# Separate stage orders for each engine, and coefficients from powers of one symmetric matrix, in a four-layer graph kernel

## The reference, cut to what matters

```python
def layer0(x): h = relu(x@w1_loop + adj@(x@w1_neigh) + b1)
               h = relu(h@w2_loop + adj@(h@w2_neigh) + b2); return (x + h) * 0.5
def layer1(x): h = x @ fc.T + fc_b; w_eff = (w*clip(d,0,1)) @ w.T      # symmetric
               8 times: h += 1/8 * (sigmoid(alpha)*0.5*(adj@h - h) + h@w_eff - h + x); return h
def layer2(x): x and x scaled by row sums of adj (once, twice), and of softmax(relu(n1@n2)); concat @ W + b
def layer3(x): attention over 256 edges (src, dst): scores, softmax over the edges of one src,
               weighted sum of values of dst, @ W_out
x = layernorm(x + layer(x))   # after each layer
```

## Time and profile before

| | us |
|---|---|
| median of 3 runs | 724.84 (724.22 to 725.11) |
| profiled execution | 727.18 |
| its span, first to last instruction | 725.3 |
| PE busy, share of the span | 597.7, 82% |
| DVE / ACT / POOL busy | 466.0 / 331.2 / 220.2 |
| mean granted PE clock | 0.901 |

### The profile page before, as it was taken

The page is one execution under the profiler, slowest core; times in us unless marked ns, Lnnn a source line. Parts: engine busy times, 40 slices in busy tenths (PEclk is TensorE's granted clock), DMA queues, the critical chain, the costliest instruction groups (busy, mean ns, idle before and its releaser), DMA issues.

```text
span 725.3 us, 9315 instructions
## 1 busy us (share of the span) xinstructions
PE 597.7 (82%) x3024; PEld 504.5 (70%) x3024; DVE 466.0 (64%) x1256; ACT 331.2 (46%) x777; POOL 220.2 (30%) x222
## 2 busy tenths in 40 slices
PE   2768849689999999996885859899999999785662
PEld 2556618558997889974774747789887998674541
DVE  6883677235464576537798779726639662678665
ACT  2661211464725367424285354663544752264132
POOL 1252502252216311232155343450552122302402
PEclk9897758789999999997898999999999999987676
DMA  7100000300000000211031110400000011001122
GB/s 221 33 0 30 0 1 0 117 1 0 2 1 1 1 1 1 83 34 59 3 114 59 58 59 1 117 1 1 1 0 1 1 67 51 0 1 59 58 58 59
DMA packets 28502, 24.61 MB, mean 34 GB/s; under 512 B 3739, under 2 KB 22683, under 8 KB 28453
## 3 DMA queue, kind: packets, MB, share of 16 engines
q1 hardware_dynamic: 27012, 19.25, 8.7%
q0 software_dynamic: 1440, 4.72, 2.1%
HBM read 15.58 MB, written 8.39 MB: 33 GB/s over the span
## 4 chain that ended last, share of the span: by engine, by line
PE 60%; DVE 28%; ACT 5%; issue 3%; POOL 2%; DMA 1%; ACTq 0%; DVEq 0%; POOLq 0%
PE bank L1260 32%; PE bank L1542 11%; DVE stats L1076 6%; PE bank L1459 5%; PE bank L1458 4%; ACT ZH L624 2%; PE bank L1434 2%; PE bank L1446 1%; PE bank L1515 1%; POOL ZL L540 1%; DVE XF L1167 1%; DVE XF L1241 1%; PE bank L1328 1%; POOL small L563 1%; DVE XF L1094 1%
## 5 line engine op out<-in xcount | busy, mean ns | idle before, releaser
L563 POOL TENSOR_TENSOR small<-small,minus_half 128x8 f32<-128x8 f32 x32 | 55.1, 1722 | 314.4 <-DVE small L1069 314.4
L540 POOL TENSOR_TENSOR ZL<-XF,ZH 128x512 fp32r<-128x512 f32 x64 | 80.9, 1299 | 105.8 <-ACT ZH L624 105.8
L624 ACT ACTIVATE ZH<-bank 128x128 fp32r<-128x128 f32 (+1 forms) x112 | 35.8, 323 | 110.4 <-PE bank L1260 109.9
L1048 DVE TENSOR_TENSOR ZL<-bank,ZH 128x128 fp32r<-128x128 f32 (+1 forms) x112 | 37.7, 345 | 69.7 <-ACT XF L624 53.4
L813 ACT ACTIVATE XF<-XF,small 128x128 f32<-128x128 f32 x128 | 52.0, 486 | 53.1 <-POOL small L565 46.8
L1260 PE MATMUL bank<-QH,YR 128*128 128x384 f32 x256 | 75.9, 337 | 0.0
L1459 PE MATMUL bank<-ZL,BTH 128*128 128x512 f32 x192 | 74.3, 418 | 0.0
L1458 PE MATMUL bank<-ZH,BTH 128*128 128x512 f32 x144 | 61.0, 423 | 2.1 <-POOL ZL L540 2.0
L1076 DVE BATCH_NORM_STATS2 stats<-XF 128x6 f32<-128x128 f32 x256 | 55.8, 281 | 2.2
L1542 PE MATMUL bank<-ZH,RH 128*128 128x512 f32 x128 | 51.1, 399 | 1.7 <-POOL ZL L540 0.8
L1542 PE MATMUL bank<-ZH,RL 128*128 128x512 f32 x128 | 50.7, 396 | 0.0
(11 more groups left out here) (280 smaller groups left out, 1535.9 us busy)
## 6 DMA issues: line engine op xcount, KB each, us to landing
XF<-in_x SPq DMA_DIRECT2D x16, 256.0 KB, 3.9
XT<-in_xT SPq DMA_DIRECT2D x16, 256.0 KB, 4.5
x_rows<-XF SPq DMA_DIRECT2D x16, 256.0 KB, 2.6
out_x<-XF SPq DMA_DIRECT2D x16, 256.0 KB, 2.8
XF<-in_adj SPq DMA_DIRECT2D x1, 1024.0 KB, 5.6
Q<-in_L_gnn_W SPq DMA_DIRECT2D x1, 448.0 KB
Z<-x_rows,ends_at POOLq DMA_INDIRECT x16, 3.5
Q<-in_L_gnn_w_neigh SPq DMA_DIRECT2D x2, 64.0 KB, 4.4
```

The lines of the kernel that those rows point to most:

```text
L540: g.tensor_tensor(lo, whole, raw(hi), ALU.subtract).then_inc(pool_done[s], 1)
L563: g.tensor_tensor(sm[:, 6, :], sm[:, 5, :], minus_half[:, :], ALU.pow).then_inc(pool_done[s], 1)
L624: return A.activation(out_, in_, ACT.Copy, **more)
L1048: ins = (v.tensor_tensor(lo, part, raw(hi), ALU.subtract) if shift is None else v.scalar_tensor_tensor(lo, part, shift, raw(hi), ALU.add, ...
```

## The change

1. in_order stays only to number the steps of the preparation (w_numbered). Each engine gets its own list of stages, own_order. For the tensor, scalar and vector lists the stages are the same as before except for powers; their places differ. In the preparation pw0, pw1, pw2 stand in place of powers, spread between neigh1, r2, conv1, edges, pair2 and neigh2, and pair2 and neigh2 of group 0 come before r3. 1.neigh1 on PE stands directly behind w.end and ahead of 0.step1. In the vector list row_sum moves into lmat.
2. Only powers of V are formed, V2, V3, V4 and V5 to V8, in three steps; V is symmetric, so it can be the transposed operand as it is. ACT scales them by binomials into VC (8 blocks). DVE adds them up with 28 scalar_tensor_tensor into SV (8 blocks), which POOL has set to scaled identities. Q_k is fc' times VC_k plus centring times SV_k: 7 products over up to three blocks at once. POOL's stage q and its wait are gone.
3. Scratch moves from X1, T1 and part of TL1 to Y1, F1 and tiles of its own (VC, SV, FJV). `load(1, 1)` has no wait, `load_t(1, 1)` waits for one_hot. In stream 1's first turn x0 waits for l3, conv1 (ACT) for picked and t_sum, pair2 (DVE) for q_t; step1 of group 0 waits for "done". The logits, picked and q_t use stream 0's banks, after conv2 of group 0.

```diff
-        adj_rows = T1[:, NB * N + 2 * E:NB * N + 2 * E + EB * N].rearrange("p (e m) -> p e m", m=N)
-        power_0 = scratch("X1", [3, D])
-        powers = scratch("T1", [(EULER_STEPS - 2) // 2, 4 * D])
+        at["F1"] = 0
+        adj_rows = scratch("F1", [EB, N])
+        power = scratch("F1", [EULER_STEPS - 1, D])
+        FCN, CENTRE, V = FJV[:, 0, :], FJV[:, 1, :], FJV[:, 2, :]
...
+        own_order = {
+            "tensor": """w.adj w.low w.w0 w.v w.pw0 0.neigh1 w.r2 w.pw1 0.conv1 w.edges 0.pair2 w.pw2 0.neigh2 w.r3 w.rt
+                w.l2_mean w.weights w.picked w.soft w.end 1.neigh1 0.step1 0.t1 1.conv1 0.step2 0.tz.0 0.tz.1
+                0.lot.0 0.tz.2 1.pair2 0.lot.1 0.tz.3 1.neigh2 0.lot.2 0.lot.3 0.giant1 1.step1 1.t1 0.giant2
+                1.step2 1.tz.0 0.t2 1.tz.1 0.l2.0 0.l2.1 0.l2.2 0.l2.3 1.lot.0 1.tz.2 1.lot.1 1.tz.3 1.lot.2 1.lot.3
+                1.giant1 0.gather 0.qv 0.score 1.giant2 0.spread 0.wout 1.t2 0.scatter 1.l2.0 1.l2.1 1.l2.2 1.l2.3
+                2.neigh1 2.conv1 2.pair2 2.neigh2 1.gather 1.qv 1.score 2.step1 1.spread 1.wout 2.t1 1.scatter
+                2.step2 2.tz.0 2.tz.1 2.lot.0 2.tz.2 3.neigh1 2.lot.1 3.conv1 2.tz.3 2.lot.2 3.pair2 3.neigh2
+                2.lot.3 2.giant1 3.step1 3.t1 2.giant2 3.step2 3.tz.0 3.tz.1 3.lot.0 3.tz.2 2.t2 3.lot.1 2.l2.0
+                2.l2.1 2.l2.2 3.tz.3 2.l2.3 3.lot.2 3.lot.3 3.giant1 3.giant2 2.gather 2.qv 3.t2 2.score 3.l2.0
+                3.l2.1 3.l2.2 3.l2.3 2.spread 2.wout 2.scatter 3.gather 3.qv 3.score 3.spread 3.wout 3.scatter""",
+            "scalar": """w.adj w.low 0.x0 w.v 0.t0 w.lmat 0.neigh1 w.pw0 w.r2 0.conv1 0.triple w.pw1 0.pair2 w.pw2 w.rt
+                0.norm.0 1.x0 1.t0 w.picked w.soft w.end 0.split1 1.neigh1 0.t1 0.split2 1.conv1 1.triple 0.tz.0
+                0.tz.1 0.lot.0 0.tz.2 1.pair2 0.lot.1 0.tz.3 0.lot.2 0.lot.3 1.norm.0 1.split1 0.split3 1.t1
+                1.split2 0.norm.1 1.tz.0 0.t2 1.tz.1 0.l2.0 0.l2.1 0.l2.2 0.l2.3 1.lot.0 1.tz.2 1.lot.1 1.tz.3
+                0.norm.2 1.lot.2 1.lot.3 0.gather 0.qv 1.split3 0.score 1.norm.1 0.wout 1.t2 1.l2.0 1.l2.1 0.norm.3
+                1.l2.2 2.x0 1.l2.3 2.t0 2.neigh1 2.conv1 2.triple 2.pair2 1.norm.2 2.norm.0 1.gather 1.qv 2.split1
+                1.score 1.wout 2.t1 2.split2 2.tz.0 2.tz.1 1.norm.3 3.x0 2.lot.0 2.tz.2 3.t0 3.neigh1 2.lot.1
+                3.conv1 2.tz.3 3.triple 2.lot.2 3.pair2 2.lot.3 3.norm.0 3.split1 2.split3 3.t1 3.split2 3.tz.0
+                3.tz.1 2.norm.1 3.lot.0 3.tz.2 2.t2 3.lot.1 2.l2.0 2.l2.1 2.l2.2 3.tz.3 2.l2.3 3.lot.2 3.lot.3
+                2.norm.2 3.split3 2.gather 3.norm.1 2.qv 3.t2 2.score 3.l2.0 3.l2.1 3.l2.2 3.l2.3 3.norm.2 2.wout
+                3.gather 3.qv 2.norm.3 3.score 3.wout 3.norm.3""",
+            "vector": """w.adj w.low w.w0 w.v w.lmat w.pw0 0.t0 0.neigh1 w.r2 w.pw1 w.edges 0.pair2 w.pw2 0.neigh2 w.r3 w.rt
+                w.one_hot w.q w.weights w.picked w.soft w.end 0.norm.0 1.t0 1.neigh1 0.step1 0.t1 0.step2 0.tz.0
+                0.tz.1 0.lot.0 0.tz.2 1.pair2 0.lot.1 0.tz.3 1.neigh2 0.lot.2 0.lot.3 1.norm.0 0.giant1 1.step1 1.t1
+                0.giant2 1.step2 0.norm.1 0.t2 1.tz.0 0.l2.0 0.l2.1 1.tz.1 0.l2.2 1.lot.0 1.tz.2 0.l2.3 1.lot.1
+                1.tz.3 0.norm.2 1.lot.2 1.lot.3 0.x3 1.giant1 0.gather 0.qv 0.score 1.giant2 0.spread 1.norm.1
+                0.wout 1.t2 0.scatter 1.l2.0 1.l2.1 0.norm.3 2.t0 2.neigh1 1.l2.2 1.l2.3 2.pair2 1.norm.2 2.neigh2
+                1.x3 1.gather 1.qv 2.norm.0 1.score 2.step1 1.spread 1.wout 2.t1 1.scatter 2.step2 2.tz.0 2.tz.1
+                2.lot.0 1.norm.3 2.tz.2 3.t0 3.neigh1 2.lot.1 2.tz.3 3.pair2 2.lot.2 3.neigh2 2.lot.3 3.norm.0
+                2.giant1 3.step1 3.t1 2.giant2 3.step2 3.tz.0 3.tz.1 2.norm.1 3.lot.0 3.tz.2 2.t2 3.lot.1 2.l2.0
+                2.l2.1 3.tz.3 2.l2.2 3.lot.2 2.l2.3 3.lot.3 2.norm.2 3.giant1 2.x3 3.giant2 2.gather 3.norm.1 2.qv
+                3.t2 2.score 3.l2.0 3.l2.1 3.l2.2 3.l2.3 3.norm.2 2.spread 2.wout 2.scatter 3.x3 3.gather 3.qv
+                2.norm.3 3.score 3.spread 3.wout 3.scatter 3.norm.3""",
+            "gpsimd": """0.x0 0.neigh1 0.conv1 0.stats.0 w.one_hot 1.x0 0.split1 1.neigh1 0.split2 1.conv1 1.stats.0 1.split1
+                0.split3 1.split2 0.stats.1 0.stats.2 0.x3 1.split3 1.stats.1 0.stats.3 2.x0 2.neigh1 2.conv1
+                1.stats.2 1.x3 2.stats.0 2.split1 2.split2 1.stats.3 3.x0 3.neigh1 3.conv1 3.stats.0 3.split1
...
+
+        def run(stages, engine=None):
+
+            for name in own_order[engine].split() if engine else in_order:
...
 
-            def w_end():
-                sync.wait_ge(w_dve_done, after(w_dve_steps, 0, "done"))
-                load(1, 1)
+            load(1, 1)
+
+            def w_one_hot():
+                sync.wait_ge(w_dve_done, after(w_dve_steps, 0, "one_hot"))
                 load_t(1, 1)
...
+            for k in range(EULER_STEPS):
+                link(g.tensor_scalar(SV[:, k, :], ident[:, :], DT + (1.0 if k == 0 else 0.0), None, ALU.mult))
             g.memset(a_pad[:, :], 0.0).then_inc(w_pool_done, 1)
...
-            def w_q():
-                gp.wait_ge(w_dve_done, after(w_dve_steps, 0, "r_lo", NB - 1))
-                for factor in factors:
-                    link(g.tensor_scalar(ident_by[factor], ident[:, :], factor, None, ALU.mult))
-                g.memset(pool_junk, 0.0).then_inc(w_pool_done, 1)
-
-            def w_end():
...
+
+            def by_choice(p, src):
+
+                k = EULER_STEPS - p
+                copy(VC[:, k, :], src, scale=float(comb(EULER_STEPS, k))).then_inc(w_act_done, 1)
...
 
                 ac.wait_ge(x_loaded[s], (turn + 1) * (16 * NB))
+                if (turn, s) == (0, 1):
+                    ac.wait_ge(w_pe_done, after(w_pe_steps, 0, "l3", NB - 1))
                 for a in range(NB):
...
+                v.tensor_reduce(row_sum, adj_sb, AX, ALU.add).then_inc(w_dve_done, 1)
...
+            def w_pw0():
+                dv.wait_ge(w_dve_done, after(w_dve_steps, 0, "row_sum"))
+                dv.wait_ge(w_pe_done, after(w_pe_steps, 0, "v2"))
+                v.tensor_copy(power[:, 0, :], w_bank[3][:, 0:D]).then_inc(w_dve_done, 1)
...
+
+            def w_sums():
+
+                nonlocal n
+                dv.wait_ge(w_pool_done, after(w_pool_steps, 0, "const"))
+                dv.wait_ge(w_dve_done, after(w_dve_steps, 0, "v8"))
+                for p in range(1, EULER_STEPS):
+                    if p > 1:
+                        dv.wait_ge(dve_chain, n)
+                    v_p = V if p == 1 else power[:, p - 2, :]
+                    for k in range(EULER_STEPS - p):
+                        v.scalar_tensor_tensor(SV[:, k, :], v_p, DT * comb(k + p, k), SV[:, k, :],
+                                               ALU.mult, ALU.add).then_inc(dve_chain, 1)
+                        n += 1
+                dv.wait_ge(dve_chain, n)
+                v.memset(tmp_c, 0.0).then_inc(w_dve_done, 1)
...
             def neigh1(turn, s):
+                if (turn, s) == (0, 1):
+                    dv.wait_ge(w_pe_done, after(w_pe_steps, 0, "l2_mean", 1))
...
             def w_r2():
+                pt.wait_ge(w_dve_done, after(w_dve_steps, 0, "v2"))
                 by_adjacency("l")
 
             def w_r3():
-                pt.wait_ge(w_dve_done, after(w_dve_steps, 0, "src_col"))
+                pt.wait_ge(w_dve_done, max(after(w_dve_steps, 0, "src_col"), after(w_dve_steps, 0, "v8")))
...
-                products(w_bank[0][:, 0:D], [(V4, power(4, 0))]).then_inc(w_pe_done, 1)
+            def w_pw0():
+                pt.wait_ge(w_dve_done, after(w_dve_steps, 0, "nv1_t"))
+                products(w_bank[3][:, 0:D], [(V, V)]).then_inc(w_pe_done, 1)
+
+            def w_pw1():
+                pt.wait_ge(w_dve_done, max(after(w_dve_steps, 0, "v2"), after(w_dve_steps, 0, "l2", NB - 1)))
+                products(w_bank[0][:, 0:D], [(power[:, 0, :], V)])
+                products(w_bank[0][:, D:2 * D], [(power[:, 0, :], power[:, 0, :])]).then_inc(w_pe_done, 1)
+
+            def w_pw2():
+                pt.wait_ge(w_dve_done, after(w_dve_steps, 0, "v4"))
+                products(w_bank[3][:, 0:D], [(power[:, 2, :], V)])
+                products(w_bank[3][:, D:4 * D], [(power[:, 2, :], power[:, 0:3, :])]).then_inc(w_pe_done, 1)
 
...
             def w_soft():
+                pt.wait_ge(dve_done[0], after(dve_steps, 0, "conv2", 1))
                 for a in range(NB):
...
             def w_q():
-                pt.wait_ge(w_pool_done, after(w_pool_steps, 0, "q"))
...
+                pt.wait_ge(dve_done[0], after(dve_steps, 0, "conv2", NB - 1))
+                pt.wait_ge(w_dve_done, max(after(w_dve_steps, 0, "log_in"), after(w_dve_steps, 0, "rowmax", NB - 1)))
                 for i in range(LOTS):
-                    for place in range(LOT):
-                        k = place * LOT + i
-                        (_, f_factor), *parts = q_parts[k]
```

(14 more changed lines are left out.)

234 lines of the change are left out of this document (115 added, 119 removed).

## The result

The changed kernel takes 718.97 us (median of 4 runs, 717.28 to 720.04) against 724.97 for the kernel before on the same chip: a ratio of 0.9903, with a 95% interval of 0.9886 to 0.9919. Five further runs in a later study gave 719.6 us and 0.9925 (0.9912 to 0.9938). The forecast was 704, with 694 to 715 for 8 in 10: right in sign, but a gain of 20.5 us was forecast and 6.0 came. The profiled execution took 717.28 us, its span 715.5, PE busy 578.1, DVE 485.9, POOL 222.5 us, clock 0.914.

What follows compares the result with a forecast made beforehand. PE bounds it (60% of the chain of waits, DVE 28%), saturated in two stretches, 118 us idle in the others. 13 + 11 − 1 − 2.5 = 20.5 us of gain from 724.84 gave 704, range 694 to 715 for 8 in 10.

Steps and rivals of the forecast that it cites:

- lead at 0.step2's end: Preparation to 0.step2: step2 ends as before with 13.5 us of stream 1 done; gain 13, ends 9 and 18.
- middle: Old 314 to 458 us: reordered stages remove PE waits, score chain 12 earlier; gain 11, ends 3 and 13.
- end: Behind 3.giant1: 2.gather moves behind 3.giant2, so gather_lo stands behind statistics; loss 2.5, ends 0 and 4.
- 0.step2 to 1.giant1: In front of 0.t2 one place fewer covers the norm: loss 1.
- my walk: Preparation, DVE queue followed stage by stage: sums from 92.7, taking 12.1; PE's products done at 132.8, bounds 128.5 to 136.
- The stretch after it is PE-bound: Behind 0.step2, with DVE at 95 of 169 us: the head start is a gain of 13.
- the middle's queue walk: Middle, DVE's queue in its new order, assuming no wait missed: 1.l2.2 and 1.l2.3 end at 386, score chain 12 earlier.
- new gaps over 5 us in sum: Sign of being wrong, in saturated stretches: the separate orders cost where the forecast put nothing.
- rival (d): Slower, by the port DVE and POOL share: a norm meeting POOL's low parts costs 3.9 more; 739 with 9 more; chance 0.08.
- norms of 6 us: Sign of being wrong: norms on DVE taking 6 us in number.
- The new wait for gather_lo behind 3.giant2: Sign of being right, at the end: PE newly waits for gather_lo, 2.48 us, behind 8 us of statistics.
- Rival (a): Only the lead stays; in the middle what one wait yields returns in the next: 13 + 3 − 3.5 = 12.5, 712; chance 0.22.

Runs made afterwards that it cites:

- old rest: Changed kernel with every engine's stages behind 0.step2 back in the order of the kernel before, new preparation and early stream 1 kept: 716.95 us.
- S and E old: Changed kernel with the old order from 0.step2 to 1.giant1 and from 2.tz.0 on, new order only between: 714.01 us.
- S old: Changed kernel with only the stages between 0.step2 and 1.giant1 back in the old order on each engine: 715.34 us.
- the changed kernel with the late 1.x0: Changed kernel with nothing altered except that POOL's 1.x0 waits for VectorE's picked stage: 714.92 us, ratio 0.9850.
- the preparation alone: Changed kernel with stream 1 starting behind 0.step2 as before and all stages after the preparation in old order: 722.84 us.
- the kernel with the late 1.x0: The 714.01 us kernel (new order only from 1.giant1 to 2.tz.0) with POOL's 1.x0 waiting for VectorE's picked stage: 707.77 us.
- the products inside the softmax: The 707.77 us kernel (POOL's 1.x0 waiting for picked) with the three w.end coefficient products taken into the softmax stage: 707.76 us.

## Why the prediction was wrong

By its own terms, in us of gain: the forecast, the two profiles set side by side, and the medians of kernels that differ in one part (725.37, 722.84, 716.95, 714.01, 715.34 and 719.60, read in the order of the last column):

```
                         forecast   profiles   medians
lead at 0.step2's end      13         11.6       8.4   (preparation 2.5, early start 5.9)
middle                     11          6.4       2.9   (old rest -> S and E old)
2.tz to 3.giant1            0          0        -1.3   (S and E old -> S old, both rows together)
end                        -2.5       -3.5
0.step2 to 1.giant1        -1         -4.6      -4.3   (S old -> changed kernel)
sum                        20.5        9.9       5.7   (span 9.8)
```

Each step of the last column is uncertain by 1 to 2 us; by the ratios it reads 3.4, 5.1, 3.0, -1.3 and -4.8. Of the profiles that of before was 2.2 us above its median and that of after 1.7 below, which is 3.9 of the difference between the two sums. I took the first into account for the level and not for the gain; the second couldn't be known. Against the second profile of before the lead is 9.5 instead of 11.6.

**The preparation: its times right, its worth not.** Edges' answer, pair2, neigh2 and the one-hot stage came 0 to 3.5 us behind my walk (sums start at 96.2, forecast 92.7), the sums took 9.7 instead of 12.1, 1.neigh1 stood behind the seven products without a gap and done was at 134.1 (132.8, bounds 128.5 to 136). One reading in that walk was wrong: the 0.27 us of the earlier trace rows lie between a sum and a tensor_scalar, not between two like instructions. The sums alone take 6.5 us, not 8.2, and the copy and the sums pay 4.2 for POOL's work, not 3.9, so the total came near by two errors of opposite sign. What the lead was worth I read against the profile of before alone: 13, of which 8.4 are left by the medians. The runs price it apart: preparation 2.5, early start 5.9 with POOL beside the sums, and 6.2 more without (by the ratios of each study 3.4, 5.1 and 5.6), so 11 to 12 for the early start when nothing is paid beside it. POOL's x0, in my sum at 3.9, is 4.2 on DVE and 5.6 to 6.2 in the time.

**The failed steps: "The stretch after it is PE-bound", and the middle's queue walk.** The first let the whole head start through a stretch and costed the reordering in it at 1, because PE was full there. It was full because transposes had another stage's work between them and their user. With the 0.l2 stages in a row some of that cover went, and 4.3 us with the new order as a whole, shown by putting the order back (2.2 to 2.9 of it in the late half). That it is the neighbours and nothing else in that order is read from the waits, not tried apart. Another 2.2 us, as the profiles have it, went because 1.neigh1 and 1.conv1, done early, had been such cover themselves. The sign I had named, new gaps over 5 us in sum, came only in part: PE's empty time there rose by 3.4 us, from 1.66 to 5.08.

In the second I walked DVE with the durations of the trace of before, l2.2 and l2.3 in 8 us. They took 14, because POOL's subtractions for group 2 now ran beside them. I had the price of this for the sums and for norm.3 and did not ask which other stages would now meet POOL's; rival (d) asked that of norms only. Leaving POOL's work out gave 6.3 us in the middle's length and 7.7 in the time (7.1 by the ratios), so my 11 was the 2.9 of the medians plus about that. Norm.0 of group 0 took 4.30 us instead of 2.13 too, beside POOL's subtractions and under cover of 1.neigh1; no norm took more than 5.11, so the sign "norms of 6 us" did not come.

The middle's mechanism failed as well as its size. I had PE's empty time fall from 30 to about 20 us. Over the whole middle it is 31.1 and 27.4 in the two profiles of before, and 27.1 to 29.3 in the ten profiles with the new order and POOL's work in it: the waits of 4.62 and 7.66 went, and so did one of 2.54 behind the score chain, but new ones came.

```profile
333.70 3.41 PE L1341 MATMUL bank<-w_out,Y 128*128 128x128 f32 x16 [4.44 <-DVE Y L1312]
```

With this one ahead of 0.wout there are 1.75 and 4.19 us inside 2.pair2, and 7.74 ahead of 1.gather where the kernel before had 5.37 ahead of 1.qv. What fell is PE's busy time for the same 557 matmuls, from 112.1 and 116.8 to between 107.6 and 111.0, with the mean granted clock at 0.91 to 0.94 instead of 0.88 to 0.90. I had no term for that, so the part of the forecast that came in there came in partly by luck.

**The rest.** 2.conv1's wait of 7.66 fell to 0.26 as forecast, and the score chain of group 0 came early. The new wait for gather_lo behind 3.giant2 came: 4.96 us.

```profile
602.61 0.58 PE L1621 MATMUL bank<-ZH,RH 128*128 128x512 f32 x1 [2.67 <-POOL ZL L583]
...
622.31 0.55 PE L1341 MATMUL bank<-TH,gH 128*128 128x256 f32 x1 [4.96 <-DVE TL L1125]
```

But the remedy I implied, the gather back ahead of 3.giant2, brought nothing by itself; together with the old order before 3.giant1 it brought 1.3 us. Of the end's 3.5 us, 1.6 are the clock: 3.giant2 in the changed kernel, then in the changed kernel with the late 1.x0 (stretches as above).

```profile
602.60:615.60 13.00, 12.99 (x50) 10.35 (x51) 3.67 (x7) 0.00 (x0) 4.01 (x3) 0.87 0.00 1
```

```profile
599.00:610.50 11.50, 11.43 (x50) 9.23 (x51) 3.62 (x7) 0.00 (x0) 4.13 (x3) 1.00 0.01 1
```

This is no matter of a single execution. With 2.gather behind 3.giant2, PE stands still for 2.67 us ahead of it; in four of six such profiles 3.giant2 then took 13.0 us at clock 0.87, in two 11.4 at 1.00. In the ten profiles where that wait is 0.42 it took 11.4 every time. The place of the gather thus costs more than the wait itself in most executions, and my sum had no term for it.

Rival (a) was nearest in time (712) and, by the medians, in the middle too: it kept 3 there, which is what they show. Its reason, that what is taken from one wait comes back in the next, fits PE's empty time. But it kept the full lead of 13 and did not have the 4.3 lost behind 0.step2.

**Open.** The profiles account for 2.4 of the 4.3 us of the old order before 1.giant1; they show 6 to 7 us for the new middle where the medians show 3; and where the single executions of the changed kernel lose up to 4 us was not found.

## What to carry to other kernels

A stretch in which the bound engine is full may be full because of its order; here moving stages in it was not free. The thing to check is whether a producer and its user have become neighbours, also by taking out what stood between them. When stages move, list for each what the GpSimd runs beside it: here a VectorE sum of two SBUF operands took 1.3 to 1.8 us instead of 0.3 to 0.75, and one wait that moved five microseconds of GpSimd work gave about 6 us, by the medians twice what the new order brought in the middle. Price a head start against the kernel with the rest of the change and no head start, since part of what it seems to win may already be in that one. And read what a part is worth from medians as well as from two profiles: here they differ by 3 us and more in single parts.

## What the hardware showed that I had not expected

Work put into a gap can raise the clock of what follows. From the last coefficient product to 0.step2's end the kernel before ran at a mean granted clock of 0.74 and 0.83 in its two profiles, with PE standing still for 6.64 and 2.80 us in between; the preparation alone ran at 0.88; in the changed kernel, where 1.neigh1 and 1.conv1 fill the gaps, the stretch is at 1.00. A wait can cost clock, too: behind 2.67 us of standing still 3.giant2 ran at 0.87 in four of six profiles, behind 0.42 us at 1.00 in all ten.

An earlier start can be lost to the clock. In the kernel with the late 1.x0 the clock rose to 1.00 during the coefficient products, at about 125 us, and 1.neigh1 began behind that, at 127.07. With the products inside the softmax 1.neigh1 began at 122.96, and PE was at the lower level from about 122.8 to 126.2 and again, after two waits for 0.split1, from 136.4 to 139.9: 1.neigh1 took 9.2 us instead of 7.7, 0.step1 was slower too, and the lead of 4.1 us was gone at 0.t1. One profile of each shows this.

Contention with POOL also hits some instructions with one SBUF input: a copy of 128x256 took 1.29 us beside POOL's subtractions and 0.29 otherwise, while four BATCH_NORM_STATS2 kept their 0.87.
